# A graph and attention block on one core: visits in 41 groups of eight instead of 81 groups of four, and a sixth batch in the second ring

## What is computed

```python
def gnn_layer(x, W, b, src, dst):
    h = x @ W.T + b
    agg = segment_sum(h[src], dst, num_segments=1250)
    return relu(agg)

# mixer
q = softmax(xn @ Wq.T, axis=-1) * 512 ** -0.5
k = softmax(xn @ Wk.T, axis=-2)
x2 = einsum('bnd,bde->bne', q, einsum('bnd,bne->bde', k, xn @ Wv.T)) + xn
mix = x2 @ W1.T @ W2.T + x2
```

## Time and profile before

| | |
|---|---|
| Median of 3 runs | 469.66 us (468.04 to 470.31) |
| The profiled execution | 469.05 us, its span 467.3 us |
| Granted TensorE clock, mean | 0.994 |
| PE / DVE / ACT / POOL busy | 96% / 67% / 32% / 14% of the span |
| `vp0` to the last visit | 86.1 to 233.7 us |
| z product starts | 246.3 us |

### The profile page before, as it was taken

One profiled execution on the slowest core, in us unless ns is written; L12 is line 12 of the kernel. 1 busy time (PEld: TensorE's weight loads), 2 busy tenths in 40 slices (PEclk: granted clock), 3 DMA queues, 4 the chain that ended last, 5 costly groups with the idle time before them and its releaser, 6 DMA issues.

```text
span 467.3 us, 6438 instructions
## 1 busy us (share of the span) xinstructions
PE 449.9 (96%) x2449; PEld 349.5 (75%) x2449; DVE 312.4 (67%) x681; ACT 150.6 (32%) x274; POOL 64.0 (14%) x108
## 2 busy tenths in 40 slices
PE   8999999999999999999999999999999999778995
PEld 4788778777777777777779999777777776454783
DVE  5995799899987888887741110444546567777972
ACT  4686454332322323242222111222141116441110
POOL 3188210000000000000004000004100000005642
PEclk9999999999999999999999999999999989999998
DMA  7902002912000000002100000004744459106791
GB/s 214 283 9 90 1 0 63 239 16 93 14 1 0 2 0 1 1 1 85 41 1 2 1 1 3 0 0 126 241 135 130 140 163 391 62 1 229 255 350 71
DMA packets 20824, 40.42 MB, mean 87 GB/s; under 512 B 2936, under 2 KB 3266, under 8 KB 20787
## 3 DMA queue, kind: packets, MB, share of 16 engines
q1 hardware_dynamic: 18547, 32.55, 22.4%
q0 software_dynamic: 2240, 7.39, 4.3%
HBM read 30.10 MB, written 10.30 MB: 86 GB/s over the span
## 4 chain that ended last, share of the span: by engine, by line
PE 85%; DVE 8%; ACT 3%; DMA 1%; issue 1%; SPq 1%; POOLq 0%; DVEq 0%; ACTq 0%
PE ps L732 47%; PE ps L1022 9%; PE ps L954 9%; PE ps L845 5%; PE ps L717 3%; PE ps L1039 2%; ACT scrap_a L1397 2%; PE ps L1148 2%; DMA RAW_K<-in_WkT 1%; PE ps L1118 1%; PE ps L877 1%; PE ps L981 1%; PE ps L766 1%; PE ps L1061 1%; PE ps L1003 1%
## 5 line engine op out<-in xcount | busy, mean ns | idle before, releaser
L1685 DVE TENSOR_TENSOR RING_S<-every_home,HOME 125x512 bf16<-125x512 f16 x64 | 43.8, 684 | 0.0
L954 PE MATMUL ps<-AT,H1H 125*128 125x416 f32 (+1 forms) x108 | 38.0, 352 | 0.0
L954 PE MATMUL ps<-AT,H1L 125*128 125x416 f32 (+1 forms) x108 | 38.0, 351 | 0.0
L1683 DVE TENSOR_TENSOR RING_D<-places,PLACES 125x440 bf16<-125x440 f16 (+3 forms) x64 | 36.4, 569 | 0.0
L1022 PE MATMUL ps<-H2H,AT 125*125 125x512 f32 x90 | 36.1, 402 | 0.0
L1022 PE MATMUL ps<-H2L,AT 125*125 125x512 f32 x90 | 35.5, 394 | 0.0
L1039 PE MATMUL ps<-WE0H 128*128 128x512 f32 x125 | 35.4, 419 | 0.0
L1753 DVE TENSOR_TENSOR ps<-ps,bias 125x512 f32<-125x512 f32 x20 | 14.0, 700 | 28.7 <-PE ps L732 28.7
L1834 DVE SCALAR_TENSOR_TENSOR ZL<-ps,ZH 128x416 fp32r<-128x416 f32 (+1 forms) x12 | 6.3, 584 | 38.7 <-ACT ZH L1350 38.7
L606 POOL TENSOR_TENSOR G2L<-RAW_G,G2H 128x512 fp32r<-128x512 f32 x4 | 5.0, 1299 | 188.4 <-ACT G2H L1167 188.4
L1039 PEld LDWEIGHTS ps<-WE0H 128*128 128x128 f32 x125 | 22.8, 197 | 3.7
(11 more groups left out here) (401 smaller groups left out, 1175.6 us busy)
## 6 DMA issues: line engine op xcount, KB each, us to landing
RAW_E<-in_experts SPq DMA_DIRECT2D x8, 1024.0 KB, 9.2
RAW_AGAIN<-in_experts SPq DMA_DIRECT2D x3, 1024.0 KB, 8.8
X<-in_x SPq DMA_DIRECT2D x1, 2240.0 KB
out_x<-X SPq DMA_DIRECT2D x10, 224.0 KB
scratch<-X SPq DMA_DIRECT2D x10, 224.0 KB
scratch<-Y SPq DMA_DIRECT2D x10, 224.0 KB
RAW_K<-in_WkT SPq DMA_DIRECT2D x4, 256.0 KB, 5.1
RAW<-in_mW2T SPq DMA_DIRECT2D x1, 1024.0 KB, 12.8
```

The lines of the kernel that those rows point to most:

```text
L954: pe.matmul(place(f), h[0:TT, k, 128 * f:128 * (f + 1)], AT[0:TT, k, c0:c1], start=(k == 0 and n == 0), stop=False)
L1683: V.tensor_tensor(hot_d(k, w), places[0:ET, 0:w].unsqueeze(1).broadcast_to([ET, BATCH, w]), PLACES[0:ET, c].unsqueeze(2).broadcast_to([ET, ...
L1685: V.tensor_tensor(hot_s(k), every_home[0:ET].unsqueeze(1).broadcast_to([ET, BATCH, 128]), HOME[0:ET, c].unsqueeze(2).broadcast_to([ET, BAT ...
```

## The change

Spots hold eight visits, all but the first: in `vp1` to `cp3` one at matmul 6 in place of two at 0 and 6, in `q` one at 0, in `x` two at 0 and 12 in place of four at 0, 6, 12 and 18, and in `h` still at 6, now in `h0` to `h2` alone. That makes 41 groups. Batches stay at four visits with their waits and counts. `IN_A` is still 17. Ring B has six slots, its targets start 1 KB later. In `h`, DVE marks two batches in a turn in place of one. All else on every engine is the same, in the same order.

```diff
--- before.py
+++ after.py
@@ -47,7 +47,7 @@
 NVB = -(-NV // BATCH) * BATCH
 HOTW = 510
 HOTD = NT * max(WIDTHS)
-RING_A, RING_B = 2, 5
+RING_A, RING_B = 2, 6
 AGAIN = 2
 WHOLE = 1.5 * 2.0 ** 23
 WARM, WARMER = 12, 8
@@ -199,27 +199,27 @@
 def visits_in_products():
 
 
-    spots = [("vp0", 6)]
+    spots = [("vp0", 6, BATCH)]
     for u in ("vp1", "vp2", "vp3", "cp0", "cp1", "cp2", "cp3"):
-        spots += [(u, n) for n in (0, 6)]
+        spots.append((u, 6, 2 * BATCH))
     for i in range(NT + 1):
         if i < NT:
-            spots += [(f"q{i}", n) for n in (0, 6)]
+            spots.append((f"q{i}", 0, 2 * BATCH))
         if i:
-            spots += [(f"x{i - 1}", n) for n in (0, 6, 12, 18)]
-    spots += [(f"h{i}", 6) for i in range(NT)]
-    found = []
-    for k, (unit, n) in enumerate(spots):
-        vs = range(BATCH * k, min(BATCH * (k + 1), NV))
-        if vs:
-            found.append((unit, n, vs))
-    assert len(found) * BATCH == NVB
+            spots += [(f"x{i - 1}", n, 2 * BATCH) for n in (0, 12)]
+    spots += [(f"h{i}", 6, 2 * BATCH) for i in range(NT)]
+    found, v = {}, 0
+    for unit, n, count in spots:
+        if v < NV:
+            found[unit, n] = range(v, min(v + count, NV))
+        v += count
+    assert v >= NV
     return found
 
 
-BATCHES = visits_in_products()
-VISITS_AT = {(unit, n): vs for unit, n, vs in BATCHES}
-IN_A = next(k for k, (unit, n, _) in enumerate(BATCHES) if (unit, n) == ("q0", 6)) + 1
+VISITS_AT = visits_in_products()
+BATCHES = [range(v, min(v + BATCH, NV)) for v in range(0, NV, BATCH)]
+IN_A = (VISITS_AT["q0", 0][-1] + 1) // BATCH
 
 
 def ring_slot(k):
@@ -341,8 +341,8 @@
         MARK_S = small("MARK_S", [128, RING_A, BATCH, 128], BF16, "a")
         MARK_D = small("MARK_D", [128, RING_A, BATCH, HOTD], BF16, "a")
         RING_S = at("RING_S", [128, RING_B, BATCH, 128], BF16, 125)
-        RING_D = at("RING_D", [128, RING_B, BATCH, HOTD], BF16, 130)
-        assert 130 + RING_B * HOTD * BATCH * 2 / KB <= 137
+        RING_D = at("RING_D", [128, RING_B, BATCH, HOTD], BF16, 131)
+        assert 131 + RING_B * HOTD * BATCH * 2 / KB <= 137.25
         start = small("start", [128, NB + 1], F16, "a")
         turns = small("turns", [128, NB], F16, "a")
         over = small("over", [128, 1], F32, "p")
@@ -1670,7 +1670,7 @@
             def mark_next(n=1):
 
                 for k in range(marked[0], min(marked[0] + n, len(BATCHES))):
-                    vs = BATCHES[k][2]
+                    vs = BATCHES[k]
                     w = max(width(ORDER[v][0]) for v in vs)
                     c = slice(BATCH * k, BATCH * (k + 1))
                     if k == 0:
@@ -1766,7 +1766,7 @@
                 if i:
                     h1_left(i - 1)
                 if marked[0] < len(BATCHES):
-                    mark_next()
+                    mark_next(2)
             h1_left(NT - 1)
             assert marked[0] >= len(BATCHES)
             dve.wait_ge(loads["pairs"], 32)
```

## The result

Over 11 executions each on the same chips, the changed kernel takes 471.68 us in the median (470.52 to 476.27) and the kernel before 468.24: **0.79% slower** (ratio 1.0079, 95% interval 1.0061 to 1.0096). The prediction was 472.8 us against a median before of 469.66, a ratio of 1.0067, and the measured time is inside its range. The profiled execution took 472.99 us, on the long side of the eleven.

The account below looks back on a forecast made before the run. TensorE, busy 96% of the span, was taken as the bound. Saving and waits, -2.6 + 0.6 + 0.3 + 1.0 + 3.8 = +3.1 us, gave 472.8 us against the median of 469.66; 8-in-10 range 470.6 to 474.8.

Parts of the forecast that it names:

- `h`: In `h1` and `h2`, batches 77 to 80 marked behind a bias: waits of 0.7, 0.9, 1.3 and 0.9, together 3.8 us.
- `x9`: At `x9` matmul 12, DVE's gapless chain from the peak of `q9` ends batch 74 late: wait of 1.0 us.
- `q0`: At `q0`, batch 16 must wait for visits to free one of ring A's two slots: wait of 0.6 us.
- The thin places: At `x0` and in `vp`, small shortages of DVE against TensorE: 0.3 us in all, bounds 0 and 1.
- the `vp` one: In `vp1` to `vp3`, DVE needs 3.45 us per product, TensorE 3.3; counted within the 0.3 us of thin places.
- The saving: All groups: 40 merges save 0.065 us each in going over and back, 2.6 us, bounds 2.4 and 3.2.
- The weighing of the weight loads: TensorE's visits: loads of 107 ns pacing them would make the saving 0 and the time 475.4 us; rejected, 2.6 kept.
- Rival 4: The granted clock falls behind the new waits: one product at 1.2 GHz adds 2.8 us, 475.6 us; chance 0.03.
- Rival 1: Marks for `q0`, `x0` and `x9` arrive in time, only the `h` waits come: +1.2, 470.9 us; chance 0.2.
- Rival 2: Both marks of each `h` turn hide and 74 precedes `x9` 12; the saving stands alone: 467.1 us; chance 0.08.
- Rival 3: DVE's order bounds every `x` tile: 0.2 us lost in nine tiles adds 1.8, 474.6 us; chance 0.12.

Follow-up runs that it names:

- experiment 1: Changed kernel with two batches (77 and 78) marked ahead of the first bias of `h`; ratio 1.0029 to the kernel before.
- experiment 2: experiment 1 plus G1 splits moved behind the mark of batch 74 and ACT's copy ahead of the rounding in `h`; ratio 0.9965 to the kernel before.
- experiment 9: experiment 2 with the visits of `q0` in two groups of four, all splits on DVE; ratio 0.9951 to the kernel before, median 466.45 us.
- experiment 7: experiment 2 with WQ and G1 splits moved from DVE to POOL and `q0` in two groups of four; ratio 1.0019 to the kernel before.
- experiment 11: Kernel before with 29 merges in `q1` to `q9` and `x` alone, G1 splits behind batch 74, ACT's copy first in `h`; ratio 0.9967.
- experiment 3: Changed kernel with groups of eight in `h0` to `h2` alone, all others of four; ratio 1.0122 to the kernel before.
- experiment 8: Changed kernel with ring B of five slots in place of six; ratio 1.0118 to the kernel before, median 474.01 us.
- experiment 6: Changed kernel with 14 useless dense matmuls ahead of the four waits of `h`; ratio 1.0070 to the kernel before.

## Why the prediction was right

**The direction and the cause held.** What bound was TensorE's path, and on it the marks that came late by DVE's order (`h`, `x9`) and by the two slots of ring A (`q0`); slots of ring B played no part. These are the places forecast, and undoing each of them took its wait away (experiments 1, 2, 9). The waits at `vp3` to `cp1` and in `x0` were not tested by an edit of their own.

**The waits, term by term.** `h`: 3.8 forecast, 3.85 found, each of the four within 0.05 us. `x9`: 1.0 forecast, 1.10 found. `q0`: 0.6 forecast, 0.73 found; I had added nothing for a semaphore's release, which the chain now puts at 0.05 us ("issue") for each wait. The thin places were undersized: 0.3 forecast with bounds 0 and 1, 1.0 found. The step that failed is the `vp` one. I saw that DVE needs 3.45 us where TensorE needs 3.3, but not that TensorE, with a crossing less, needs 3.2 (groups at 90.83, 94.06 and 97.26), nor that this shortage adds up over the products from `vp2` on until `vp3`, `cp0` and `cp1` wait 0.64 us together. And I applied the two slots of ring A to `q0` alone. They already hold up batch 3, by the 0.89 us shown above, and after that DVE runs without a gap: its low part of `vp2` begins 97.41 - 85.50 = 11.91 us behind the start of `vp0`, where it was 97.52 - 86.14 = 11.38 before. By an estimate from these rows the shortage without this lateness would have cost 0.64 - 0.53, some 0.1 us. No run separates the two: experiment 7 takes the splits off DVE, but there POOL stretches the marks.

**The saving was undersized too.** 2.6 us forecast at 0.065 a merge, 3.07 found at 0.077, inside the bounds of 2.4 and 3.2. Most of the difference lies in the visit: I took 0.055 us for each, in groups of eight they start 0.052 apart, and 0.283 - 4 x 0.052 is 0.075. The two errors, 1.0 us more waits and 0.5 us more saving, in part cancel, which is luck: 3.1 forecast, 3.6 found without the clock. That the absolute time, 471.68 us, lies under the forecast of 472.8 comes from the kernel before, whose median was 1.4 us lower this time.

**The weighing of the weight loads held.** The Trainium skill (TensorE: Matmul & The Clock Gate, section LDWEIGHTS) has a load of 128 columns take 107 ns. Had that paced the visits, the saving would have been 0; experiment 11 has 2.24 us for 29 merges.

**Rival 4 came beside the forecast.** I gave the fallen clock 0.03, with the argument that a gap of 1.21 us had left the clock at 1.00. That argument failed: it priced one gap, where here four gaps of 0.7 to 1.3 us fall within 8 us. The clock fell in all four profiled executions that held these four waits (the changed kernel twice, experiments 3 and 8), and in none of the others in `h`; even the 2.0 us wait of experiment 7, standing alone, left it. Nor did I ask what had gone ahead of the fall that the kernel before shows itself. It comes at 379.4 us, behind a stretch in which TensorE was busy for 3.11 of 3.40 us, so a long idle time isn't what it needs:

```profile
376.00:379.40 3.40, 3.11 (x25) 2.63 (x23) 2.39 (x12) 0.86 (x3) 0.00 (x0) 1.00 0.48 151
379.40:382.80 3.40, 3.35 (x10) 2.78 (x10) 1.89 (x7) 0.00 (x0) 0.00 (x0) 0.50 0.50 113
```

The six matmuls of 2.91 us that I took for the price stand in the second of these stretches. The rule in the Trainium skill (TensorE: Matmul & The Clock Gate, section A second HAM failure mode), by which short idles between groups of matmuls make the clock swing, was the better guide. The fall's price here, 1.6 us, was under my 2.8. The clock doesn't fall in every execution: one of the seventeen of the changed kernel, of 471.45 us, has a mean granted clock of 1.00 over its whole span, where one such fall would leave 0.996. How often it falls stays open. The stretch is 3.6 us longer than before without the fall and 5.2 with it, and the ratios of the changed kernel, 1.0079 and 1.0081 (3.7 and 3.8 us), lie near the lower of the two. Nor is the changed kernel's mean clock over whole executions, 0.9935 and 0.9947, far from the 0.9938 to 0.9951 of the kernel before. The ratios of experiments 3 and 8 (5.7 and 5.5 us) lie above both, with four executions each and a mean clock of 0.991 and 0.992.

**Rivals 1 to 3.** The waits at `q0` and `x9` didn't vanish (1), the marks didn't hide (2), and between `x1` and `x8` no group waits (3): DVE keeps ahead there.

## What to carry to other kernels

A merge that saves a crossing also moves work forward in time: list for each merged piece what must be ready, and when its producer's program order lets it be. Here the same 40 merges gave 0.8% more time or 0.35% less, by where a few marks stood in DVE's order. Give the idle time of a producer the work that will be waited for (DVE idled 2.5 us ahead of the bias) before buying buffers. Ask of each ring by itself whether its slots bind: the sixth slot of ring B was never what a mark waited for, while the two of ring A held up the marks at `vp1` and `q0`.

## What was unexpected of the hardware

- Four idle stretches of TensorE, waits of 0.7 to 1.3 us within 8 us, were followed in all four profiled executions that held them by 3.4 us at the granted clock of 0.50, 1.2 GHz, with dense matmuls of 512 columns 0.43 us apart in place of 0.233; 14 useless matmuls in the same gaps kept it at 1.00 (experiment 6). A single gap of some 2 us in experiment 7 did not lower it.
- POOL subtractions over SBUF stretch DVE's 16-bit comparisons from 0.61 and 0.68 us to 1.16 and 1.77, and leave a DVE instruction with a PSUM input at 0.67 (experiment 7).
- Going from float32 matmuls to a group of small bf16 ones and back costs time of its own: each merge of two groups of four into one of eight took off 0.077 us on average (experiment 11, 2.24 us for 29 merges).
